# A state-space layer's convolution kernel from half its lags, in a fused two-layer Trainium2 kernel

## What is computed

```python
def _s4_kernel(Lambda, p, q, B, Ct, step, L):        # L = 512
    Omega = jnp.exp(-2j * jnp.pi * (jnp.arange(L) / L))
    ...
    at_roots = c * (k00 - k01 * (1.0 / (1.0 + k11)) * k10)
    return jnp.fft.ifft(at_roots, L).real
...
K = _s4_kernel(Lambda, p, q, B, Ct, step, L).astype(u.dtype)
y = jnp.fft.irfft(jnp.fft.rfft(u, n=n) * jnp.fft.rfft(K, n=n), n=n)[..., :L]
return y + D[0] * u
...
xn = _layernorm(x, axis=-1)
x = x + _L0_attn_ref(xn, ...) + _L0_ffn_ref(xn, W_gate, W_up, W_down)
xn = _layernorm(x, axis=-1)
x = x + _L1_attn_ref(xn, ...) + _L1_ffn_ref(xn, ...)
```

## Time and profile before

| | |
|---|---|
| three timed runs | 1087.91, 1088.5, 1088.92 us; median 1088.5 |
| the profiled execution's own time | 1087.31 us |
| its span, first to last instruction | 1085.5 us (1.8 us lie around it) |
| TensorE busy | 1080.9 us, 100% of the span |
| VectorE, ScalarE, GpSimd busy | 744.9, 562.2, 741.8 us (69, 52 and 68%) |
| granted TensorE clock | 1.00 of full speed over the span |
| loads and stores | 54.39 MB, mean 50 GB/s |

### The profile page before, as it was taken

How to read it: one execution, slowest core, us unless ns; L and a number is a source line. 1 busy time by engine, 2 the same in 40 slices (tenths; PEclk the granted TensorE clock), 3 DMA queues, 4 the chain that set the end, 5 groups by cost and what they waited for, 6 DMA issues and landing times.

```text
span 1085.5 us, 21396 instructions
## 1 busy us (share of the span) xinstructions
PE 1080.9 (100%) x6376; PEld 956.8 (88%) x6376; DVE 744.9 (69%) x1842; ACT 562.2 (52%) x1690; POOL 741.8 (68%) x1030
## 2 busy tenths in 40 slices
PE   9999999999999999999999999999999999999999
PEld 8888878998998898889888988898899889988987
DVE  7598955567767666776667666666667666676675
ACT  4445221134745555556456646654665466555663
POOL 4777567997938962977487648864795579379911
DMA  5111342101200210111021101110111012001102
GB/s 179 35 59 48 98 137 68 64 30 40 79 20 20 79 40 21 44 56 39 20 59 40 39 19 59 40 39 19 60 48 49 0 60 72 25 18 57 44 1 78
DMA packets 23875, 54.39 MB, mean 50 GB/s; under 512 B 3424, under 2 KB 4000, under 8 KB 23648
## 3 DMA queue, kind: packets, MB, share of 16 engines
q1 hardware_dynamic: 23776, 53.37, 15.4%
HBM read 51.26 MB, written 2.10 MB: 49 GB/s over the span
## 4 chain that ended last, share of the span: by engine, by line
PE 96%; POOL 3%; DVE 1%; issue 0%; ACT 0%; POOLq 0%; DVEq 0%
PE banks L186 28%; PE banks L187 28%; PE banks L188 28%; PE banks L2072 4%; PE banks L2091 3%; PE banks L2063 3%; POOL acc L534 1%; PE banks L1313 1%; POOL form_lo L1637 0%; PE banks L1175 0%; DVE mixed L881 0%; PE banks L1363 0%; POOL form_hi L1635 0%; POOL tT_lo L540 0%; POOL wc_lo L488 0%
## 5 line engine op out<-in xcount | busy, mean ns | idle before, releaser
L1637 POOL TENSOR_TENSOR form_lo<-wqk_stage,form_hi 128x256 fp32r<-128x256 f32 x192 | 142.0, 740 | 16.0
L1691 POOL TENSOR_SCALAR vf_hi<-wvo_stage 128x512 fp32r<-128x512 f32 (+1 forms) x48 | 26.4, 550 | 167.2 <-PE banks L188 153.9
L1971 ACT ACTIVATE prob<-prob,top 128x128 f32<-128x128 f32 (+1 forms) x256 | 115.7, 460 | 15.7 <-DVE top L2000 15.6
L1977 ACT ACTIVATE prob<-prob,inv 128x128 f32<-128x128 f32 (+1 forms) x256 | 102.7, 451 | 38.4 <-DVE inv L2006 38.4
L2000 DVE CUSTOM_DVE_ANT_0 prob<-banks,mask 128x128 f32<-128x128 f32 (+1 forms) x256 | 81.3, 355 | 59.4 <-PE banks L188 46.4
L2018 DVE TENSOR_TENSOR acc<-acc,banks 128x512 f32<-128x512 f32 x129 | 86.8, 677 | 35.9 <-PE banks L188 35.7
L186 PE MATMUL banks<-tT_hi,form_hi 128*128 128x512 f32 x256 | 105.6, 412 | 0.0
L187 PE MATMUL banks<-tT_lo,form_hi 128*128 128x512 f32 x256 | 100.2, 391 | 0.0
L188 PE MATMUL banks<-tT_hi,form_lo 128*128 128x512 f32 x256 | 100.1, 391 | 0.0
L186 PE MATMUL banks<-wo_hi,oT_hi 128*128 128x512 f32 x240 | 95.9, 400 | 0.0
L188 PE MATMUL banks<-wo_hi,oT_lo 128*128 128x512 f32 x240 | 93.6, 390 | 0.0
(11 more groups left out here) (351 smaller groups left out, 3726.7 us busy)
## 6 DMA issues: line engine op xcount, KB each, us to landing
wqk_stage<-in_w_qk SPq DMA_DIRECT2D x32, 512.0 KB, 3.2
wvo_stage<-in_w_v SPq DMA_DIRECT2D x34, 256.0 KB, 2.6
wvo_stage<-in_w_o SPq DMA_DIRECT2D x32, 256.0 KB, 2.7
wd_stage<-in_w_down SPq DMA_DIRECT2D x22, 256.0 KB, 2.6
gu_stage<-in_w_gu SPq DMA_DIRECT2D x10, 512.0 KB, 3.2
acc<-in_x SPq DMA_DIRECT2D x8, 256.0 KB, 4.7
out<-acc SPq DMA_DIRECT2D x7, 256.0 KB, 2.0
tab<-in_w_comb SPq DMA_DIRECT2D x1, 1300.0 KB, 6.0
```

The lines of the kernel that those rows point to most:

```text
L1637: nc.gpsimd.tensor_tensor(form_lo[:, part], src[:, :], as_f32(form_hi[:, part]), ALU.subtract).then_inc(form_ready, 1)
L1971: ins = nc.scalar.activation(pr, pr, ACT.Exp, bias=top[:, n % 2, r:r + 1], scale=-1.0, accum_out=total[:, n % 2, r:r + 1])
L1977: ins = nc.scalar.activation(pr, pr, ACT.Copy, scale=inv[:, n % 2, r:r + 1])
```

## The change

- The tables hold lags 0 to 256 only (`LAGS` is 257), and the Nyquist cosine has a row of its own. Cosine sums are even and sine sums are odd about lag 256, so lag 512-l follows from the same two sums as lag l.
- TensorE makes the sine (odd) sum in one bank by two matmuls of 257 columns, and the cosine (even) sum in another by two, plus one matmul with a contraction of one row for Nyquist: five plain float32 matmuls of 257 columns in place of four of 512.
- ScalarE copies the odd sum into `s4` row block 7. VectorE adds it to the even sum for lags 0 to 256, and for lags 257 to 511 subtracts, reading both in reverse: two operations in place of one copy.
- Since row block 7 is now used, the bias is loaded there later: after the lag sum and both VectorE operations, just ahead of `w_comb`. The tables are 658 KB (128 x 1285 numbers) where they were 1024 KB.
- The single-row operation at the end of `phases` writes `s4[0:1, 6, 0:P]` in place of row 0 of `uv`.

```diff
+LAGS = DM // 2 + 1
...
-        sp.dma_start(tab[:, 0:2 * FT * DM], tables).then_inc(tab_loaded, 16)
-        sp.wait_ge(cauchy_done, 1)
-        sp.dma_start(bias, b_base.partition_broadcast(P)).then_inc(bias_loaded, 16)
+        sp.dma_start(tab[:, 0:(2 * FT + 1) * LAGS], tables).then_inc(tab_loaded, 16)
         for n in range(4, NF):
             load_wd(n)
 
         sp.wait_ge(toep_done, 1)
+        sp.wait_ge(toep_copied, 2)
+        sp.dma_start(bias, b_base.partition_broadcast(P)).then_inc(bias_loaded, 16)
         sp.dma_start(wc_stage, w_comb.rearrange("k p n -> p k n")).then_inc(wc_loaded, 16)
...
         second_hi(range(0, 4))
+        act.wait_ge(odd_done, 1)
+        nc.scalar.activation(s4[:, 7, 0:LAGS], banks[:, G + 2, 0:LAGS], ACT.Copy).then_inc(odd_copied, 1)
         act.wait_ge(toep_ready, 1)
...
-            link(nc.vector.tensor_scalar(uv[0:1, 1, 0], sin_t[0:1, 0, 0:P], cs[0:1, 8, FT:FT + 1], None, ALU.mult))
+            link(nc.vector.tensor_scalar(s4[0:1, 6, 0:P], nyquist[:, 0:P], cs[0:1, 8, FT:FT + 1], None, ALU.mult))
...
             dve.wait_ge(toep_done, 1)
-            nc.vector.tensor_copy(s4[:, 5, :], banks[:, G + 1, :]).then_inc(toep_copied, 1)
+            even, odd = banks[:, G + 1, 0:LAGS], s4[:, 7, 0:LAGS]
+            dve.wait_ge(odd_copied, 1)
+            nc.vector.tensor_tensor(s4[:, 5, 0:LAGS], even, odd, ALU.add).then_inc(toep_copied, 1)
+            nc.vector.tensor_tensor(s4[:, 5, LAGS:DM], even[:, LAGS - 2:0:-1], odd[:, LAGS - 2:0:-1],
+                                    ALU.subtract).then_inc(toep_copied, 1)
+            dve.wait_ge(toep_copied, 2)
             dve.wait_ge(toep_masked, 1)
...
-        for i, table in enumerate((cos_t, sin_t)):
-            for t in range(FT):
-                ins = nc.tensor.matmul(banks[:, G + 1, :], uv[:, i, t], table[:, t, :],
-                                       start=i + t == 0, stop=i * FT + t == 2 * FT - 1)
-        ins.then_inc(toep_done, 1)
+        for t in range(FT):
+            ins = nc.tensor.matmul(banks[:, G + 2, 0:LAGS], uv[:, 1, t], sin_t[:, t, :], start=t == 0, stop=t == FT - 1)
+        ins.then_inc(odd_done, 1)
+        for t in range(FT):
+            nc.tensor.matmul(banks[:, G + 1, 0:LAGS], uv[:, 0, t], cos_t[:, t, :], start=t == 0, stop=False)
+        nc.tensor.matmul(banks[:, G + 1, 0:LAGS], s4[0:1, 6, 0:P], nyquist, start=False, stop=True).then_inc(toep_done, 1)
```

More of the change, by code:

```diff
@@ L209, in layer0 @@
     xh = hF
-    cos_t = tab[:, 0:FT * DM].rearrange("p (t l) -> p t l", t=FT)
-    sin_t = tab[:, FT * DM:2 * FT * DM].rearrange("p (t l) -> p t l", t=FT)
+    cos_t, sin_t = (tab[:, i * FT * LAGS:(i + 1) * FT * LAGS].rearrange("p (t l) -> p t l", t=FT) for i in range(2))
+    nyquist = tab[0:1, 2 * FT * LAGS:(2 * FT + 1) * LAGS]
     wc_stage = tab[:, 0:KD * WC].rearrange("p (k n) -> p k n", k=KD)
@@ L281, in layer0 @@
     toep_copied = sem("toep_copied")
+    odd_copied = sem("odd_copied")
+    odd_done = sem("odd_done")
     toep_masked = sem("toep_masked")
@@ L2233, in constants @@
     cos, sin = np.cos(turn), np.sin(turn)
-    sin[0] = np.cos(np.pi * np.arange(DM))
-    tables = np.stack([cos, sin]).astype(np.float32)
-    tables = tables.reshape(2, FT, P, DM).transpose(2, 0, 1, 3).reshape(P, 2 * FT * DM)
+    tables = np.zeros((P, 2 * FT + 1, LAGS), np.float32)
+    tables[:, 0:FT] = cos[:, 0:LAGS].reshape(FT, P, LAGS).transpose(1, 0, 2)
+    tables[:, FT:2 * FT] = sin[:, 0:LAGS].reshape(FT, P, LAGS).transpose(1, 0, 2)
+    tables[0, 2 * FT] = np.cos(np.pi * np.arange(LAGS))
+    tables = tables.reshape(P, (2 * FT + 1) * LAGS)
     mask = np.zeros((P, 2 * P), np.float32)
```

## The result

| | before | after |
|---|---|---|
| median of 15 runs | 1088.36 us | 1091.02 us |
| lowest to highest | 1087.38 to 1088.92 | 1089.01 to 1092.61 |
| profiled execution, its span | 1087.31, 1085.5 us | 1091.77, 1089.9 us |

The ratio is 1.0024, 95% interval 1.0017 to 1.0031. The change made the kernel slower by 2.7 us where a gain of 0.7 was forecast, and its time now varies by 3.6 us from run to run, where before it was 1.5. The profiled execution lies in the upper half of its runs. In 8 of the 15 executions the mean granted clock is 0.998 or 0.997, and their median is 1091.7; in the other seven it is 1.000, with a median of 1089.7. So a loss of 1.3 us stands without any fall of the clock.

A forecast was written before the change was run, and what follows sets the result against it. TensorE, 0.20 us behind a transfer queue at chunk 13, was taken as the bound. Terms -1.27 (matmuls) + 0.68 (bias) - 0.10 (GpSimd-VectorE overlap) = -0.7 us gave 1088.5 - 0.7 = 1087.8 us, range 1086.6 to 1089.1.

The forecast's parts named there:

- What bounds the kernel: TensorE, 1080.9 of 1085.5 us busy, waits 0.20 us at chunk 13 for GpSimd, which block 11's queued transfer holds up.
- The lag matmuls: In the lag sum, ten passes of 257 columns replace eight of 512, saving 1.27 us; one-row product priced as full.
- The lag block, tables and `phases`: Copies behind the lag sum, smaller tables and the phases work cost nothing; slack 10.8 us for toep_lo, 5.2 for phases.
- The bias load: Moved ahead of w_comb in the transfer queue, its 256 KB delay block 11 by 0.68 us, at most 1.3.
- The rival "slower": Bias broadcast ahead of w_comb drains slowly, costing over 1.27 us, up to 1092.2 us total; chance 0.05 including the columns.
- the columns: Rival at the lag sum: 257-column passes cost as much as 512, giving 1090.0 us; within a shared chance of 0.05.
- What is late next: At chunk 13, block 11 lands at 157.37; the chunk starts 0.69 us earlier, TensorE's wait grows from 0.20 to 0.78.
- the meeting of GpSimd and VectorE: In GpSimd's stretch before chunk 13, overlap with a VectorE operation shifts from block 12 to block 11, winning 0.10 us.
- The second place: At 217.54 to 232.78 us, the chain through GpSimd's bias additions shifts with chunk 13; nothing lost or won.

The follow-up runs named there:

- full rows: Changed kernel with the bias load behind block 14 and the Nyquist product over all 128 rows, the added ones zeros: 1087.07 us against 1087.8, ratio 0.9991.

## Why the prediction was wrong

**What bounds the kernel: right.** The chain was the one named: lag matmuls, block 8, issue of `w_comb`, landing of block 11, GpSimd's stretch, chunk 13. Taking a row block of `w_comb` (2.4 us) out of that stretch frees TensorE there, in three kernels.

**The lag matmuls: right in kind, a term mis-sized.** 1.27 was forecast and 0.87 measured. A pass of 257 columns takes 0.217 us, as scaled. The failing part is "the product with one row of contraction is counted as a full one ... above I know no row that makes it dearer": it cost 0.82 us and not 0.43, and full rows gave the 0.40 back. Nor did the queue gain all of what TensorE gained: block 11 was issued 0.67 us earlier from the start of the lag sum, not 0.87 (and not 1.27), because the hi part of block 8 now took GpSimd 0.89 us where it had taken 0.70.

**The lag block, tables and `phases`: right in that they cost nothing.** `toep_lo` was ready at 147.61 (it had been 148.04), more than 11 us before its use. `phases` ended at 139.5, 2.6 us later from the same origin than before, with several VectorE operations drawn out, which was not foreseen; 2.6 us of slack stayed.

**The bias load: the step that failed.** The prediction said "So 256 KB behind a full queue took 0.68 us" and carried that price to a place in front of the queue. Behind `w_comb` it is right as far as can be told (0.66 between medians, 0.67 in the traces). In front of `w_comb` block 11 took 8.1 us to land and not 5.0, 3.1 more where 0.68 was put; in three other traces with the bias there it took 7.0, 7.4 and 7.4. The range's upper bound for this term, 1.3 us, came from the old place too. The rival "slower" had the right place and effect, a load ahead of `w_comb` that makes block 11 late. Its reason, that all engines read the same 2 KB, is at most a part, since a plain load and `w_expb` in that place did it too, in some executions. It was given 0.05, together with the columns, because "most of those 5.0 us it stood behind the tables". That row could not tell the two apart: the load may be slow and still end soon after a longer one under which it ran.

**What is late next: half.** The wait at chunk 13 was foreseen to grow from 0.20 to 0.78; it grew to 2.88. That a wait of this length could cost clock was not in the prediction at all: +1.54 us in the profiled execution. Nor was chunk 15, where TensorE waits next as soon as less is lost at chunk 13. The small term of -0.10 for the meeting of GpSimd and VectorE was -0.52, since the meeting fell away altogether.

**The second place: right.** From the transposes on the two traces run in parallel, 4.4 us apart, through that place to the end.

**What stays open.** Why a second small load directly ahead of the 1.3 MB one slows the transfers, and only there. Shown: it takes no broadcast (plain load, `w_expb` first), it varies from run to run, the same load 5 us earlier or just behind costs at most its bytes, and the traces have either a dip of the rate or a remnant that moves at the busy share of a single engine. A cause inside the transfer engines was not found.

## What to carry to other kernels

A transfer's price belongs to its place in the queue: take it from a row of the same place, and treat "landed soon after the one ahead" as hidden, not as cheap. Before moving a load, look for who stands behind it in the queue and how much slack the consumer of that has; here it was 0.20 us, and a saving in front of such a point is worth nothing until the point itself is eased. When an edit makes TensorE wait a few microseconds, count the half-speed matmuls that can follow it as well. And look past the first wait: here easing it a little moved the loss to chunk 15.

## What was new about the hardware

- A plain float32 product with one row of contraction between products of 128 rows took 0.82 us for 257 columns with the gaps at its ends; the same with 128 rows, 127 of them zeros, 0.42. The loads of its weights were no longer or shorter for it (0.18 and 0.19 us).
- After TensorE had stood idle for 2.9 us, eight matmuls ran at a granted clock of 0.51 (its lower level, 1.2 GHz) and cost 1.54 us. With 2.37 us idle on the weight loads the clock fell in one trace and not in another.
- The order of three loads in one queue (256 KB, 256 KB, 1.3 MB against 256 KB, 1.3 MB, 256 KB, the same bytes) changed the median by about 1 us and the spread from 1.6 to 4.6 us.
